# Merge and second feed-forward pass in one block, batch 0 ahead of batch 1, bias on PE, first load in two halves

## The reference

```python
x = x + 0.5 * ffn(layernorm(x))           # x: (2, 1024, 128) float32
x = x + attention(layernorm(x))
x = x + 0.5 * ffn(layernorm(x))           # the same ffn weights again

def attention(x):                         # 16 heads of 8, causal
    q, k, v = split(x @ W_attn + b_attn)
    s = q @ k.T
    s = s - s.mean(-1)
    s = s / (abs(s).mean(-1) + 1e-6) * score_gain
    s = where(causal, s, -1000)
    r = maximum(s, 0) ** 4
    att = r / (r.sum(-1) + 1e-6)
    return (att @ v) @ W_proj + b_proj

def ffn(x):                               # 8 experts of 64, 4 groups of 2, top 2 of the best 2 groups
    scores = sigmoid(x @ gate_w) + gate_bias
    idx, w = top2(scores, groups)         # w normalised, times 2.5
    y = sum_k w[k] * (silu(x @ w_gate[idx[k]]) * (x @ w_up[idx[k]])) @ w_down[idx[k]]
    return y + (silu(x @ sw_gate) * (x @ sw_up)) @ sw_down
```

## Time and profile before

| | |
|---|---|
| median of three runs | 477.9 us (477.0 to 478.38) |
| profiled execution, its own time | 477.65 us |
| its span, first to last instruction | 475.9 us |
| busy: PE, DVE, ACT, POOL | 409.9, 396.4, 323.8, 281.0 us |
| mean granted clock of PE | 0.974 |
| first pass and before / projections / attention / merge / second pass start at | 0 / 91.8 / 116.6 / 376.9 / 401.7 us |

### The profile page before, as it was taken

How to read it: one execution, slowest core, us unless ns; L and a number is a source line. 1 busy time by engine, 2 the same in 40 slices (tenths; PEclk the granted TensorE clock), 3 DMA queues, 4 the chain that set the end, 5 groups by cost and what they waited for, 6 DMA issues and landing times. The chain is left out here.

```text
span 475.9 us, 13631 instructions
## 1 busy us (share of the span) xinstructions
PE 409.9 (86%) x5040; PEld 192.3 (40%) x5040; DVE 396.4 (83%) x928; ACT 323.8 (68%) x584; POOL 281.0 (59%) x205
## 2 busy tenths in 40 slices
PE   0779999761889999999999999999999875889996
PEld 0323444341244444444444444444444453334442
DVE  5886555886899999999999999999999988675443
ACT  3323222554799999999999999999999704422221
POOL 5960000044689999999999999999999800000000
PEclk9989999987899999999999999999999998899999
DMA  4300000005661504205105032051003100000001
GB/s 117 89 1 0 1 0 0 1 26 106 212 122 40 81 9 78 48 4 100 25 26 87 15 70 55 3 101 25 3 6 80 41 11 0 2 0 22 0 22 44
DMA packets 18140, 19.92 MB, mean 42 GB/s; under 512 B 4808, under 2 KB 10536, under 8 KB 18088
## 3 DMA queue, kind: packets, MB, share of 16 engines
q1 hardware_dynamic: 17736, 19.11, 18.9%
q10 hardware_dynamic: 352, 0.07, 0.1%
HBM read 13.02 MB, written 6.03 MB: 40 GB/s over the span
## 5 line engine op out<-in xcount | busy, mean ns | idle before, releaser
L1249 POOL TENSOR_TENSOR arena<-arena 128x1024 f32<-128x1024 f32 (+1 forms) x144 | 240.7, 1704 | 20.3 <-ACT arena L1221 19.6
L1182 DVE SCALAR_TENSOR_TENSOR arena<-bank,masks 128x512 f32<-128x512 f32 x288 | 179.9, 681 | 8.2 <-PE bank L1088 8.2
L1221 ACT ACTIVATE arena<-arena 128x1024 f32<-128x1024 f32 (+1 forms) x160 | 147.9, 959 | 1.1 <-DVE arena L1182 0.2
L1088 PE MATMUL bank<-Q,K 128*32 128x512 bf16 (+3 forms) x1536 | 96.5, 331 | 23.4 <-DMA K<-k_parts 10.3
L1211 ACT ACTIVATE bank<-bank 128x1024 f32<-128x1024 f32 (+5 forms) x144 | 90.0, 625 | 8.0 <-PE bank L1088 7.4
L1088 PE MATMUL bank<-K,Q 128*32 128x512 bf16 (+3 forms) x1536 | 93.0, 329 | 0.0
L1188 DVE TENSOR_SCALAR_CACHE_REDUCE bank<-bank 128x896 f32<-128x896 f32 (+4 forms) x112 | 83.9, 778 | 0.0
L1125 PE MATMUL bank<-arena,Vq 128*32 128x512 f32 (+3 forms) x768 | 77.0, 486 | 0.0
L624 ACT ACTIVATE arena<-bank 128x512 f32<-128x512 f32 x40 | 23.9, 597 | 75.3 <-PE bank L499 75.3
L1088 PEld LDWEIGHTS bank<-Q,K 128*32 128x32 bf16 x1536 | 37.2, 96 | 89.5 <-issue 22.5
L725 DVE TENSOR_TENSOR arena<-arena,bank 128x512 f32<-128x512 f32 x40 | 27.4, 685 | 41.7 <-PE bank L503 41.6
(11 more groups left out here) (122 smaller groups left out, 349.1 us busy)
## 6 DMA issues: line engine op xcount, KB each, us to landing
Q<-q_parts SPq DMA_DIRECT2D x24, 192.0 KB
K<-k_parts SPq DMA_DIRECT2D x16, 128.0 KB
att<-arena SPq DMA_DIRECT2D x28, 64.0 KB, 1.6
K<-k_parts SPq DMA_DIRECT2D x8, 192.0 KB
X<-in_L_attn_x SPq DMA_DIRECT2D x4, 256.0 KB, 4.3
K<-k_parts SPq DMA_DIRECT2D x16, 64.0 KB
out_x<-X SPq DMA_DIRECT2D x4, 256.0 KB, 2.3
q_parts<-arena SPq DMA_DIRECT2D x3, 256.0 KB
```

The costliest lines, as they stand in the source:

```text
L1088: last = nc.tensor.matmul(m.bank[j:j + 32, at + lo:at + hi], left[par][:, g, blk * P + j:blk * P + j + 32], right[par][:, g, s0:s0 + hi - ...
L1182: nc.vector.scalar_tensor_tensor(Y(r, g)[:, y0:y0 + SPAN], m.bank[:, at:at + SPAN], 0.0, mask, ALU.max, ALU.mult).then_inc(relu_done, 1)
L1221: nc.scalar.activation(z, Y(r, g)[:, tile_low(r) - off(r):T - off(r)], ACT.Square)\
L1249: nc.gpsimd.tensor_tensor(z, z, z, ALU.mult).then_inc(fourth_p, 1)
```

## The change

The classes and functions of the merge and of "f2" become one class, Finish, which runs at the end of the attention block; there is no second-pass block any more.

- POOL's addition of the bias to X goes. Before each projection PE now writes the bias into the same bank (identity times bp), and the projection accumulates on it.
- The first load is split: load_quad is called for heads 0 and 1, and then for heads 2 and 3, with a semaphore each; PE waits for the second at step (0, 2).
- turn_upper(0) moves into the last quad, between steps (4, 2) and (4, 3). turn_upper(1) stands ahead of the leftover pieces. The bias and spread of spans 0 and 1 stand ahead of the last power piece.
- On DVE batch 0 goes first: both spans are divided, added and normalised before batch 1's invert. slope moves ahead of the quads and squares its value, and invert loses one instruction.
- The copies of the last quad's rows to the numerators are all issued by SP (before, half by ACT).
- The pass is written out: 20 items of gate and up, LEAD of them ahead, with the shared expert first in each span (ORDER). hid holds six products; weights and down have one bank each. Routing is for 8 tiles at the start and 8 during steps 7 to 9. Batch 1's projection, add, norm, transposes and logits stand between steps 0 and 7.
- POOL zeroes wT in the attention block.

```diff
 # project_qkv, POOL
-            nc.gpsimd.tensor_tensor(m.X[:, :, :], m.X[:, :, :], m.bp[:, :].unsqueeze(1).to_broadcast([P, NT, C]),
-                                    ALU.add)
 # project_qkv, SP
-            load_quad(nc, m, sp, q_dram, k_dram, 0, 0)
+            load_quad(nc, m, sp, q_dram, k_dram, 0, 0, range(FIRST_HEADS), m.first_heads_loaded)
+            load_quad(nc, m, sp, q_dram, k_dram, 0, 0, range(FIRST_HEADS, G))
 # attention, PE
+                    if last_quad(q) and (r, g) == (NR - 1, 2):
+                        pe.wait_ge(upper_a, q * NA + count(by_a, (NR - 1, 0)))
+                        finish.turn_upper(pe, 0)
...
-            merge.turn_upper(pe, 0)
+            finish.turn_upper(pe, 1)
             for what, r in (("relu", 3), ("power", 3), ("relu", 4)):
                 for piece in pieces(NQUAD - 1, what, r):
                     add_piece(*piece)
-            merge.turn_upper(pe, 1)
+            finish.project_bias(pe, 0)
+            finish.project_bias(pe, 1)
+            finish.spread_inverse(pe, 0)
+            finish.spread_inverse(pe, 1)
             for piece in pieces(NQUAD - 1, "power", 4):
                 add_piece(*piece)
-            merge.tensor(pe, sums, sums_out, NQUAD)
+            finish.project(pe, 0)
+            finish.project(pe, 1)
+            finish.pick_last_quad(pe, sums, sums_out)
+            finish.tensor(pe)
+    LEAD, HELD = 5, 6
+    ORDER = [NCH, 0, 1, 2, 3]
+    def new_items(self, n):
+        upto = lambda k: self.LEAD if k < 0 else min(self.LAST, max(self.LEAD + 2 * (k + 1) // 3, k + 3))
+        return range(upto(n - 1), upto(n))
+    def project_bias(self, pe, i):
+        for k in range(TPS):
+            self.nc.tensor.matmul(self.proj_ps[i][:, k * P:(k + 1) * P], self.m.ident[:, :], self.m.bp[:, :],
+                                  start=(k == 0), stop=True, skip_group_check=True)
 # Finish.tensor; item(r) waits for silu and product r - 2, down(n) of an expert for scaled(n)
+        transpose(0); transpose(1); logits(0)
+        item(0); turn_scores(0); item(1); item(2)
+        self.spread_inverse(pe, 2)
+        item(3); turn_weights(0); item(4)
+        for n in range(self.LAST):
+            if self.routed(n):
+                spread_weights(n)
+            for r in self.new_items(n):
+                item(r)
+            if n and not self.routed(n):
+                turn_back(self.span_of(n) - 1)
+            down(n)
+            if n == 0:
+                self.project_bias_after(pe, 2)      # waits for divide(2)
+                self.project(pe, 2)
+                pe.wait_ge(self.wT_ready, self.PER_B)
+                self.spread_inverse(pe, 3)
+            if n == 1:
+                self.project_bias_after(pe, 3)      # waits for divide(3)
+                self.project(pe, 3)
+            if n == 4: transpose(2)
+            if n == 5:
+                pe.wait_ge(s.xnT_ready, 3)
+                transpose(3)
+            if n == 6: logits(1)
+            if n == 7: turn_scores(1)
+            if n == 9: turn_weights(1)
+        turn_back(NSPAN - 1)
 # Finish.scalar
+        nc.scalar.activation(m.table[:, 1:2], m.eps[:, :], ACT.Sqrt)
+        root(0)
+        nc.scalar.activation(m.table[:, 2:3], m.eps[:, :], ACT.Sigmoid)
+        norm_last_tile(nc, m, s, act, 0); norm_last_tile(nc, m, s, act, 1)
+        take(0); take(1); sigmoid(0)
+        for r in range(4): item(r)
+        take_weights(0); item(4)
+        for n in range(self.LAST):
+            if n and not self.routed(n): take_out(self.span_of(n) - 1)
+            for r in self.new_items(n): item(r)
+            if n == 3:
+                nc.scalar.activation(m.table[:, 3:4], m.eps[:, :], ACT.Sqrt)
+                root(1)
+            if n == 4: norm_last_tile(nc, m, s, act, 2); norm_last_tile(nc, m, s, act, 3)
+            if n == 5: take(2)
+            if n == 6:
+                take(3)
+                nc.scalar.activation(m.table[:, 4:5], m.eps[:, :], ACT.Sigmoid)
+                sigmoid(1)
+            if n == 9: take_weights(1)
+        take_out(NSPAN - 1)
 # Finish.vector
+        invert(0); divide(0); divide(1)
+        add_attention(0); add_attention(1)
+        norm_vector(nc, m, s, dve, 0)
+        invert(1)
+        scores(0); item(0)
+        pick_groups(now); item(1)
+        pick_experts(now); item(2)
+        weigh(now); item(3)
+        divide(2); item(4)
+        for n in range(self.LAST):
+            if self.routed(n): scale(n)
+            for r in self.new_items(n): item(r)
+            if n % HCH == 1 and n > 1: add_to_x(self.span_of(n) - 1)
+            if n == 1: add_attention(2); divide(3)
+            if n == 2: add_attention(3)
+            if n == 3: norm_vector(nc, m, s, dve, 1)
+            if n == 7: scores(1); pick_groups(later)
+            if n == 8: pick_experts(later)
+            if n == 9: weigh(later)
+        add_to_x(NSPAN - 1)
```

More of the change, by code:

```diff
@@ L1053, in _ @@
             quads(sp, body)
-            merge.load(sp, att_dram)
+            finish.load(sp, att_dram)
             sp.wait_ge(sums_out, NQUAD)
-            merge.load_last_quad(sp, sums, range(G // 2))
+            finish.load_last_quad(sp, sums)
+            finish.store(sp)
         @block.tensor
@@ L1342, in scalar, with spread_inverse @@
-    def scalar(self, act):
-        nc, m = self.nc, self.m
-        nc.scalar.activation(m.table[:, :], m.eps[:, :], ACT.Sqrt)
-        act.wait_ge(self.following.moments_ready, 1)
-        norm_root(nc, m, self.following, act, 0)
-        for i in range(NSPAN // B):
-            norm_last_tile(nc, m, self.following, act, i)
-        for i in range(NSPAN // B):
-            norm_take(nc, m, self.following, act, i)
+    def spread_inverse(self, pe, i):
+        b = self.half_of(i)
+        pe.wait_ge(self.rden_ready, b + 1)
+        per = QUARTERS // self.PER_B
+        for k in range(per):
+            n = i % self.PER_B * per + k
+            last = self.nc.tensor.matmul(self.spread_ps[i][:, k * QT:(k + 1) * QT], self.m.spread[:, n, b, :],
+                                         self.m.den[b][:, :], start=True, stop=True)
+        last.then_inc(self.spread_ready, 1)
@@ new lines, in pick_last_quad @@
+    def pick_last_quad(self, pe, sums, sums_out):
+        pe.wait_ge(sums_out, NQUAD)
+        for n in range(QUARTERS):
+            for k, into in ((0, self.den_ps), (1, self.upper_ps[B - 1])):
+                half, at = n * QT // SPAN, n * QT % SPAN
+                last = self.nc.tensor.matmul(into[n * HB:(n + 1) * HB, :], self.m.pick[:, half, k, :],
+                                             sums[:, at:at + QT], start=(k == 0), stop=True, skip_group_check=True)
+        last.then_inc(self.picked, 1)
@@ L1352, in vector @@
     def vector(self, dve):
-        nc, m = self.nc, self.m
-        link = Chain(dve, self.chain)
+        nc, m, s, link = self.nc, self.m, self.norm, self.link
+        spans = lambda half: range(self.PER_B * half, self.PER_B * (half + 1))
         def invert(b):
@@ L1395, in vector, with add_to_x @@
+        def add_to_x(i):
+            dve.wait_ge(self.yt_ready, i + 1)
+            xs = m.X[:, i * TPS:(i + 1) * TPS, :].rearrange("p n c -> p (n c)")
+            nc.vector.tensor_tensor(xs, self.back_ps, xs, ALU.add).then_inc(self.x_added, 1)
+        now, later = slice(0, NT // B), slice(NT // B, NT)
         invert(0)
@@ L1397, in vector @@
         divide(1)
+        add_attention(0)
+        add_attention(1)
+        norm_vector(nc, m, s, dve, 0)
         invert(1)
-        add_to_x(0)
-        divide(2)
-        add_to_x(1)
-        divide(3)
-        norm_vector(nc, m, self.following, dve, 0)
-        add_to_x(2)
-        add_to_x(3)
+        scores(0)
+        item(0)
+        pick_groups(now)
+        item(1)
+        pick_experts(now)
+        item(2)
+        weigh(now)
+        item(3)
+        divide(2)
+        item(4)
+        for n in range(self.LAST):
+            if self.routed(n):
+                scale(n)
+            for r in self.new_items(n):
+                item(r)
+            if n % HCH == 1 and n > 1:
+                add_to_x(self.span_of(n) - 1)
+            if n == 1:
+                add_attention(2)
+                divide(3)
+            if n == 2:
+                add_attention(3)
+            if n == 3:
+                norm_vector(nc, m, s, dve, 1)
+            if n == 7:
+                scores(1)
+                pick_groups(later)
+            if n == 8:
+                pick_experts(later)
+            if n == 9:
+                weigh(later)
+        add_to_x(NSPAN - 1)
 _INS = ['L0_attn_x', 'L0_attn_W_attn', 'L0_attn_b_attn', 'L0_attn_W_proj', 'L0_attn_b_proj', 'L0_attn_score_gain',
```

375 lines of the change are left out of this document (300 added, 75 removed).

## The result

| | before | after |
|---|---|---|
| median | 477.8 us (477.0 to 478.4, four executions) | 484.5 us (482.1 to 485.6, four) |
| ratio | | 1.0135, 95% interval 1.01 to 1.0171 |
| profiled execution, its span | 477.65, 475.9 us | 484.81, 483.1 us |
| mean granted clock of PE | 0.974 | 0.975 |

Slower, as forecast, and by more: the forecast was +1.7 us, the medians differ by 6.7, the two profiled executions by 7.2. The mean granted clock is the same before and after and so says nothing here: what counts is where the clock is low, and the profile of before has low stretches (0.50 in 32 to 34 and in 104 to 106) that the profile after does not have.

What follows compares the result with a forecast made beforehand. DVE was taken to bound attention and PE the end of the second pass. Pass +6.9 and front −5.2 gave +1.7 on 477.65, so 479.4 us; the case's own range was 476 to 482, the whole range 472 to 484.5.

Steps and rivals of the forecast that it cites:

- The front, −5.2: Start of attention: no POOL bias add and a halved first load move the first matmul from 119.62 to 114.4.
- The rival of a late second half: First load: eight more issues delay the second half to 120.2, front gives 2.8 to 3.5, total 481.5; chance 0.08.
- The list of waits: Second pass: PE's waits, mostly for DVE's order, sum to 15.2 us, 16.2 with nine restarts.
- The rival in which the pass stays PE's: Middle of the pass: DVE keeps ahead of PE, saving 9.75 us for 469.7, half of it 474.5; chance 0.22.
- 65.1 + 16.2 = 81.3: Second pass from 396.75: PE's own work plus its waits, in us, ending at 478.05 against 471.15, 6.9 later.
- The late first product: Tail: first expert product forecast at 396.75 on the old clock, against 407.57 before, a gain of 10.8.
- the late weights: Second pass: batch 0's routing weights forecast ready at 407.3, with PE waiting 2.45 us for them.
- the clock's rival: Pass: PE's clock falls to 0.50 after new waits; 481 for one fall, 484.5 for three; chance 0.18.
- the prediction's own sign of being wrong: Pass: forecast is wrong if it takes under 76 us or PE's clock reads 0.50 inside it.
- 484.5 for three: Total time in us if PE's clock falls three times in the pass.
- Its price of 1.7: Cost in us of each clock fall, from some 3.4 us of half-speed work, half of the 402 to 407 stretch.
- a bar between 2.67 us (held) and 3.62 us (fell): Old merge: clock stayed 1.00 after PE's 2.67 us idle, was 0.50 after 3.62; new waits 3.2, 2.45, 2.8, 2.6 lie between.

Runs made afterwards that it cites:

- e6: Kernel before with only the first load split in halves, POOL's bias addition kept: 475.9 us, ratio 0.9946.
- e5: Kernel before with only the bias moved from POOL to PE, the first load kept single: 476.8 us, ratio 0.9969.
- e4: Changed kernel with DVE reordered: span 3's divide behind scale(1), its add behind scale(3), batch 1's later work one step later: 477.3 us, ratio 0.9978.
- e10: Changed kernel with DVE reordered, five unread matmuls, item 13 ahead of batch 1's weight turn, late weights spread early in two banks: 471.5 us, ratio 0.9864.
- e9: Changed kernel with two unread matmuls ahead of the second turn of the weights only: 485.0 us, ratio 1.0136.
- e8: Kernel before with PE's bias, the split first load and four unread matmuls at the merge's end: 472.6 us, ratio 0.9868.
- e2: Changed kernel with the old front: POOL's bias addition and a single first load, no bias matmuls on PE: 485.9 us, ratio 1.0154.
- e3: Changed kernel with eleven unread matmuls at five places where PE waits: 479.6 us, ratio 1.0016.

## Why the prediction was right in direction and short in size

**The front, −5.2: right.** It gave 5.60, by most of the steps argued: loads out at 106.21 (forecast 106.4), DVE leaving at 113.7 (114.1), block-bound start at 114.02 (114.4), the third head at 117.39 without a wait. The rival of a late second half is refuted by that row and by e6. One row came out right for a reason that the prediction does not give: POOL's subtraction starts at 105.16 (forecast 105.2), 4.32 earlier than before, where the prediction derives 2.4; 1.70 of the other 1.92 matches the fall that no longer slows PE's products for batch 1 (e5, e6). The Trainium skill's "SBUF — State Buffer", Who interferes with whom, says that a DVE instruction with two SBUF inputs contends with a GpSimd instruction that reads SBUF; the one-column add agrees (3.25 us beside POOL's addition, 0.16 without), and so does the merge's product L1635 (1.17 beside POOL, 0.48 alone).

**The list of waits: right in place and order, a little too long.** Forecast and measured: weights 2.45 and 1.93, span 3's bias 2.8 and 2.48, down(3) 2.6 and 2.25, down(6) 1.0 and 1.07, down(8) 1.15 and 0.57, down(9) 1.2 and 0.66, weights of batch 1 1.75 and 1.28, the last two scales 2.0 and 1.91. That is 14.95 against 12.15. The rival in which the pass stays PE's is refuted, and e4 shows the cause by moving it: the two middle waits vanish with DVE's order.

**The sum's wrong step: "65.1 + 16.2 = 81.3", which takes all of PE's work at the full clock.** The pass took 85.64 us and began 1.46 late. The falls of the profiled execution are priced by the same instructions in executions where the clock held: the transposes to the first up product 6.93 us (387.55 to 394.48) against 4.65 in e10; the turn of the weights to span 2's bias 4.72 against 3.02; down(3) to down(4) 4.59 against 2.89 (in e9); the second turn of the weights to the down product behind it 4.24 against 2.80 (e9). That is 2.28 + 1.70 + 1.70 + 1.44 = 7.1 us. The late first product and the late weights (409.65 on the old clock, forecast 407.3) are the first of these. Taken from 484.81 it leaves 477.7, an estimate that adds prices from several executions, and the time of before, which has a fall of its own (1.3 by e8). The forecast, made without falls, lies 1.7 above that: its waits are 2.8 too long and its front 0.4 too small, and against that some 1.5 us of the pass stand in none of its terms.

So the clock's rival is what happened, and the prediction's own sign of being wrong, a clock of 0.50 inside the pass, came true; but the rival was given 0.18. That its "484.5 for three" is the measured time, and that the stated range just holds the median (484.47, under an upper end of 484.5; the profiled execution, 484.81, lies outside), is luck: there were four falls, on waits shorter than forecast. Its price of 1.7 is what the falls inside the pass cost, though half of the 402 to 407 stretch, from which it says it comes, is 2.5 us of half-speed work and not 3.4.

The error was to read a bar between 2.67 us (held) and 3.62 us (fell) from one row on either side. Of the new waits 3.2 and 2.8 lie between these, while 2.45 and 2.6 lie under both, and the sum gives none of them a fall. The runs show falls behind waits of 1.28, 1.93 and 2.25 us and none behind a 2.48, and the other way round in e9 for the last three: a wait of this length is a chance of a fall, not a yes or no. The Trainium skill's "TensorE: Matmul & The Clock Gate", HAM oscillation, tells of a kernel whose bursts of matmuls start at the lower clock after every wait, with waits of some 3 to 5 us. The trace agrees with the warning, but shorter waits were enough here, and not every one was followed by a fall.

**What the forecast did not weigh:** that its two halves work against each other. The bias on PE frees 2.6 us in front of attention (e5) and, by the comparison with e2, takes some 3.3 back in the merge and the pass, where PE's list is the path; that is an estimate from two executions with different falls. It was in the sum as PE time (2.0 and a share of 3.9), but never set against the front's gain as one trade.

**What stays open.** What decides which wait is followed by a fall; no run here isolates it. How much a merged pass would gain with the bias neither on PE's path nor on POOL beside the projections was not tried. e9's time does not support the clock's price by itself; its trace does, for one execution.

## What to carry to other kernels

When a change cuts a dense row of matmuls into bursts, price each new wait twice: once as idle time, and once as a chance of a fall of the clock, here 1.4 to 2.3 us each, even behind waits of 1.28 and 1.93 us. Such waits can be tested cheaply with matmuls that nobody reads; where they help, move the late engine's work out of the way (7 us here by order alone) and fill only what remains. And before moving work from an engine with slack to the one that ends the chain, follow it to every place where it will stand, not only to the place that it leaves.

## What the runs showed of the hardware that was not expected

The granted clock does not repeat from execution to execution of one program, and the times scatter with it: the changed kernel's four executions lie between 482.1 and 485.6 us and e3's ten between 477.7 (clock 0.984) and 482.3 (0.975), while e8's six stay within 472.2 to 473.7 (0.982 to 0.987). In the changed kernel's four the mean clock alone does not order them (482.1 and 484.8 both at 0.975). And added matmuls made the kernel faster: some 10 us of work that nobody reads saved 5 us (e3).
